# Gated cross-attention block: staging part of one unit's rows earlier, and adding a mask by VectorE

## What is computed

```python
ln = layernorm(latents)              # the 512 rows; xn is the same of the 32 context rows
q = (ln @ Wq), kv = concat([xn @ Wkv, ln @ Wkv])      # 16 heads of 64
sim = einsum('bhid,bhjd->bhij', rmsnorm(q) * scale, rmsnorm(k))
sim = where(padded_mask, sim, -max)  # padded_mask: the context's mask, then ones for the own rows
out = einsum('bhij,bhjd->bhid', softmax(sim), v) ... @ Wout + bout
x = x + tanh(g_xattn) * out
x = x + tanh(g_ffn) * top2_experts(layernorm(x))      # 8 experts, two chosen for each row
```

## Time and profile before

| | us |
|---|---|
| three runs | 344.81, 341.92, 344.61 |
| median | 344.61 |
| the profiled execution's own time | 345.44 |
| its span (first to last instruction) | 343.5 |
| PE busy | 303.0 (88%) |
| DVE busy | 271.5 (79%) |
| POOL busy | 268.0 (78%) |
| ACT busy | 203.2 (59%) |

### The profile page before, as it was taken

The page is one execution under the profiler, slowest core; times in us unless marked ns, Lnnn a source line. Parts: engine busy times, 40 slices in busy tenths (PEclk is TensorE's granted clock), DMA queues, the critical chain, the costliest instruction groups (busy, mean ns, idle before and its releaser), DMA issues.

```text
span 343.5 us, 8712 instructions
## 1 busy us (share of the span) xinstructions
PE 303.0 (88%) x3321; PEld 185.0 (54%) x3321; DVE 271.5 (79%) x516; ACT 203.2 (59%) x353; POOL 268.0 (78%) x203
## 2 busy tenths in 40 slices
PE   0567588896999999999999999999988799999993
PEld 0233143454465555565555556688866575655552
DVE  3897868995698899899898876954827976898994
ACT  2463746764576656767755756466773466665551
POOL 8699886897498999999998996745983449677652
PEclk9996859997899999999999999999999999999997
DMA  6406322167310812613515429370100000001001
GB/s 175 143 1 141 62 31 44 33 149 167 75 44 16 179 46 44 157 36 78 126 35 127 93 55 252 67 221 29 40 10 2 1 3 0 2 3 31 2 0 32
DMA packets 33723, 23.62 MB, mean 69 GB/s; under 512 B 10834, under 2 KB 33170, under 8 KB 33682
## 3 DMA queue, kind: packets, MB, share of 16 engines
q1 hardware_dynamic: 32738, 23.03, 29.3%
q10 hardware_dynamic: 944, 0.04, 0.2%
HBM read 5.87 MB, written 0.52 MB: 19 GB/s over the span
## 4 chain that ended last, share of the span: by engine, by line
PE 59%; POOL 14%; issue 9%; DVE 9%; ACT 5%; DMA 2%; POOLq 0%; SPq 0%; DVEq 0%; ACTq 0%
PE big L1532 8%; PE big L1533 7%; POOL p_lo L634 7%; PE o_ps L1368 5%; PE big L1387 5%; PE o_ps L1362 5%; PE o_ps L1363 4%; PE pj L1339 4%; PE tv L1375 3%; POOL rms_r L498 2%; PE pj L1298 2%; DVE nm_main L997 2%; PE tv L1322 2%; PE pj L1299 1%; PE pj L1300 1%
## 5 line engine op out<-in xcount | busy, mean ns | idle before, releaser
L599 POOL TENSOR_TENSOR p_lo<-p 128x1024 f16<-128x1024 f32 x64 | 121.8, 1914 | 12.3 <-ACT p L795 12.3
L795 ACT ACTIVATE p<-big 128x1024 f32<-128x1024 f32 x64 | 65.6, 1025 | 46.3 <-PE big L1533 46.3
L997 DVE TENSOR_REDUCE nm_main<-big 128x2 f32<-128x1024 f32 x64 | 78.2, 1221 | 18.0 <-PE big L1387 17.1
L498 POOL TENSOR_TENSOR rms_r<-meansq,power 128x8 f32<-128x8 f32 x32 | 52.3, 1637 | 17.6 <-DVE meansq L971 17.5
L634 POOL TENSOR_TENSOR p_lo<-p,p_lo 128x512 f16<-128x512 f32 x32 | 37.1, 1159 | 30.3 <-ACT p_lo L876 29.4
L1532 PE MATMUL big<-w 128*128 128x512 f16 x128 | 49.3, 385 | 1.9 <-ACT p L795 1.6
L1533 PE MATMUL big<-w 68*128 68x512 f16 x128 | 49.2, 384 | 0.0
L1362 PE MATMUL o_ps<-v,p 128*128 128x65 f16 x512 | 40.7, 194 | 0.0
L1363 PE MATMUL o_ps<-v,p 128*128 128x64 f16 x512 | 40.6, 195 | 0.0
L1362 PEld LDWEIGHTS o_ps<-v,p 128*128 128x128 bf16 x512 | 35.9, 99 | 6.9 <-issue 3.9
L1363 PEld LDWEIGHTS o_ps<-v,p 128*128 128x128 bf16 x512 | 34.5, 98 | 3.3 <-issue 0.3
(11 more groups left out here) (228 smaller groups left out, 714.6 us busy)
## 6 DMA issues: line engine op xcount, KB each, us to landing
w<-hl SPq DMA_DIRECT2D x32, 256.0 KB, 4.1
w<-hl SPq DMA_DIRECT2D x32, 128.0 KB, 3.7
pc_st<-pc_hi SPq DMA_DIRECT2D x64, 32.0 KB, 1.9
pc_st<-pc_lo SPq DMA_DIRECT2D x32, 32.0 KB, 1.9
hl<-n_kernel_gating_EDF_dram SPq DMA_DIRECT2D x1, 1024.0 KB, 6.5
hl<-L_ffn_kernel_up_EDF_dram SPq DMA_DIRECT2D x1, 1024.0 KB, 5.5
o_sb<-in_L_xattn_Wkv_dram SPq DMA_DIRECT2D x2, 384.0 KB, 6.8
x_sb<-in_x_dram SPq DMA_DIRECT2D x2, 256.0 KB, 3.7
```

What stands on the lines that cost most here:

```text
L498: nc.gpsimd.tensor_tensor(rms_r[:, tau % QT, :], meansq[:, tau % QT, :], power[:, 0:8], ALU.pow).then_inc(rr_ok, 1)
L599: nc.gpsimd.tensor_tensor(p_lo[m % NP][:, :], p[m % NP][:, :], p_hi[m % NP], ALU.subtract).then_inc(plo_ok, 1)
L795: nc.scalar.activation(p[n % NP][:, :], st_ps, ACT.Exp).then_inc(exp_ok, 1)
L997: nc.vector.tensor_reduce(nm_main[:, u % 2, 2 * c:2 * c + 2, q], s2_ps.rearrange("p (k n) -> p k n", k=2), AX_X, ALU.max, negate=True).the ...
```

## The change

Two things change. SP stages unit 1's four DMAs of high halves in slot -1, ahead of the six of `Vst`; the four others, with low halves, are issued in slot 2 as before, behind the stack. And `context_scores` loses the product with the mask: the first of the eight products of 64 columns starts the bank, and DVE adds the mask in place in the bank ahead of its reduction, with a semaphore `cm_ok` between. For that the mask's row lies on all 128 partitions in 32 bits (its DMA reads it once for each partition), and the row of ones goes, with its memset on POOL.

```diff
-        mask_u8 = sb("mask_u8", [1, BC], U8)
-        mask_row = sb("mask_row", [1, B, C], BF16)
+        mask_u8 = sb("mask_u8", [P, BC], U8)
+        mask_row = sb("mask_row", [P, B, C], F32)
...
-        ones_row = sb("ones_row", [1, P], BF16)
...
-        W_AT = {(FIRST, 2)[u] if u < 2 else 8 * u - 8: u for u in range(UNITS)}
+        W_AT = {(FIRST, -1)[u] if u < 2 else 8 * u - 8: u for u in range(UNITS)}
+
+        W_LO_AT = {2 if u == 1 else n: u for n, u in W_AT.items()}
...
-            sp.dma_start(mask_u8[:, :], mask.rearrange("b c -> (b c)").unsqueeze(0)).then_inc(mask_in, 16)
+            sp.dma_start(mask_u8[:, :], mask.rearrange("b c -> (b c)").partition_broadcast(P)).then_inc(mask_in, 16)
...
                         sp.dma_start(w1[DH:P, 0:2, odd, :], hl[rows, 0, 0:2, :]).then_inc(w1_ok[u % 2], 16)
+                if n in W_LO_AT:
+                    u = W_LO_AT[n]
+                    w1, w2, hl = W1[u % 2], W2[u % 2], HL[u % 2]
                     need_lo(sp, QT * (u + 1))
...
-            nc.gpsimd.memset(ones_row[:, :], 1.0)
...
             def context_maxima(u):
                 dve.wait_ge(cs_ok, u + 1)
+                if u == 0:
+                    dve.wait_ge(mask_ok, 1)
+                sc = o_ps[0][:, :].rearrange("p (k c) -> p k c", c=C)
+                nc.vector.tensor_tensor(sc, sc, mask_row[:, batch(u), :].unsqueeze(1).broadcast_to([P, HG * QT, C]),
+                                        ALU.add).then_inc(cm_ok, 1)
+                dve.wait_ge(cm_ok, u + 1)
...
                 else:
-                    pe.wait_ge(mask_ok, 1)
                     pe.wait_ge(kc2_ok, 2)
-                nc.tensor.matmul(o_ps[0][:, :].rearrange("p (k c) -> p k c", c=C), ones_row[:, :],
-                                 mask_row[:, batch(u), :].unsqueeze(1).broadcast_to([1, HG * QT, C]), start=True, stop=False,
-                                 skip_group_check=True)
...
-                                                start=False, stop=True, skip_group_check=True)
+                                                start=c == 0 and q == 0, stop=True, skip_group_check=True)
```

More of the change, by code:

```diff
@@ L207, in flamingo_gated_block @@
         pcst_ok = [sem(f"pcst_ok{h}") for h in range(HG)]
-        kc2_z, kc2_ok = sem("kc2_z"), sem("kc2_ok")
+        kc2_z, kc2_ok, cm_ok = sem("kc2_z"), sem("kc2_ok"), sem("cm_ok")
         def need(eng, s, count):
```

## The result

The changed kernel takes 338.58 us as the median of four runs (338.50 to 338.94), beside 344.06 us for the kernel before (four runs, 341.92 to 344.81). The ratio is 0.9838, with a 95% interval of 0.9804 to 0.9871: 1.6% faster. The profiled execution took 338.54 us with a span of 336.7 us, 6.8 less than the 343.5 before.

What follows compares the result with a forecast made beforehand. PE was taken to bound the kernel from about 85 to 210 us, after a 3.01 us hole. Gains 5.71 + 0.2 + 0.3 + 0.19 - 0.35 = 6.05 us from the 344.61 median gave 338.6 us, range 335.6 to 342.0.

Steps and rivals of the forecast that it cites:

- Staging, -5.71 us: At PE's hole from 80.41 us: earlier high-half DMAs save 5.71 us, 3.01 of idling and 2.70 of low clock.
- The margin of 0.2 us: Unit 3's high halves on ACT: the last staging DMA lands at 78.5 us, 0.2 us before ACT is ready at 78.67.
- the rival of a hole left over: Part of the second rival: 1 us of hole stays at 80 us, 339.6 with the clock kept, 342.3 without.
- Mask in units 3 to 5, -0.07 each: Slot 13 and its counterparts: of PE's 0.42 us only 0.07 is left per unit at the projection into `pj`.
- Mask in unit 2, -0.07: Slot 13: the same 0.07 us gain as units 3 to 5, with DVE's pair still starting at 103.57 us.
- Unit 6, -0.19: L1418 alone decides there, comes 0.23 us late, and 0.19 of PE's 0.42 us is kept.
- Unit 7, +0.35: L1418 has 0.44 us to spare and comes 0.77 late, so PE's 0.42 becomes a loss of 0.35 us.
- Unit 1, 0: First slots, where DVE sets the pace: no mask gain taken, between 0 and 0.42 us.
- Unit 0, -0.2: Product in a stretch of clock 0.52: a gain of 0.2 us taken, between 0 and 0.5.
- The first (DVE hides all): Rival: PE keeps 0.42 us in all seven units after unit 0, 8.85 us gained, 335.8 us; chance 0.09.
- The second: Rival: the hole at 80 us stays wholly (344.3 us) or as 1 us (339.6 or 342.3); chance 0.14.
- The third: Slower rival: the mask addition is held up beside POOL, 0.76 us more each; 343.2 us, 348.6 or 359 with low clock; chance 0.05.

Runs made afterwards that it cites:

- the repetition: The changed kernel run again with no edit: 338.44 us beside 344.34 for the kernel before, ratio 0.9827.
- Staging alone: The kernel before with only unit 1's four high-half DMAs moved to slot -1, the mask still PE's product: 339.37 us, ratio 0.9843.
- mask alone: The changed kernel with all eight staging DMAs of unit 1 in slot 2 again: 343.79 us, ratio 0.9988.
- half of the staging: The changed kernel with two of unit 1's four high-half DMAs moved back behind the stack: 339.83 us, ratio 0.9875.
- product in unit 7: The changed kernel with the mask made by PE's product again in unit 7 alone: 339.05 us, ratio 0.9855.
- turned later: The changed kernel with PE's turning of the maxima, and ACT's copy of the result, one step later: 341.88 us, ratio 0.9920.
- no mask in the maxima: The changed kernel without DVE's mask addition and without PE's product, so context row maxima are taken unmasked: 337.50 us, ratio 0.9796.
- mask added twice: The changed kernel with DVE's mask addition, semaphore included, made two times: 344.63 us, ratio 1.0009 to the kernel before.
- addition in SBUF: The changed kernel with one more DVE addition of the same size, all in SBUF and read by nobody: 345.81 us, ratio 1.0019.

## Why the prediction was right, and where not

The forecast was 338.6 us, and 338.58 was measured. That it is so near is in part luck. The forecast gain was 6.0 us from a median of 344.61; with the fourth run that median is 344.06, and the measured gain is 5.5, or 5.9 (344.34 - 338.44) in the repetition. In the two profiles of the changed kernel slots 0 to 60 are 5.3 and 5.9 us shorter than before, so the profiles can't decide between them. The staging was right as a mechanism and in size; the mask's small terms are right in part, and unit 2 and unit 7 spoil their sum. Point by point:

**Staging, -5.71 us**, from the same instructions eight slots later. Staging alone gives -5.70 (5.20 and 0.50). The hole, the ACT wait behind it and the landing as its cause are confirmed by mask alone and by half of the staging. The margin of 0.2 us was mis-sized: it is 2.0 us, and 1.0 in the second profile. The working let the last DMA land 5.3 us behind its issue as before, and it took 4.0; so the rival of a hole left over was further away than I thought. The low clock behind a hole is no fixed price: 2.7 us before, 1.5 us in mask alone, none behind a hole of 1.0 us. The sum took it from one execution; by the medians, staging alone brings 5.0 us (344.34 - 339.37).

**Mask in units 3 to 5, -0.07 each.** Measured -0.10. PE's 0.42 us is confirmed to the hundredth (24.16 - 23.74), so the 0.10 beyond the product's own 0.32 is real; that it goes on the change of rows, or on the drain that the prediction cites for it, no run shows separately. DVE's 0.73 is, too: 0.72 from start to start, and 0.73 for a second one. So is the 0.06 us that the working put, without a row, between DVE's merge and PE: 0.05 in unit 2 (99.18 - 99.13) and 0.06 in unit 7 (220.06 - 220.00). The working went in two steps, 0.19 kept at the turning and 0.07 at the projection into `pj`; measured are 0.19 (0.42 less the 0.23 of slot 22) and 0.10. Only what I said would be seen was wrong: no idle time of 0.35 us stands before the projection. By the working itself only 0.12 would be left there, as 0.23 is lost at L1423; the trace of unit 3 shows 0.15 us of idle time before L1423, and the projection starts 0.42 us behind the first of its slot's scores (124.96 - 124.54), where 0.32 is usual (79.64 - 79.32).

**Mask in unit 2, -0.07.** Here a step failed: I read DVE's time of 103.57 us from a trace in which the hole stood ahead of it. Without the hole DVE is 0.30 us later there, for POOL, and the unit became 0.21 us longer than with the staging alone (24.38 - 24.17). That the removal of a hole moves everything behind it by the same amount, on every engine, was the tacit assumption; POOL "keeps pace, with little to spare" was written down and not followed up.

**Unit 6, -0.19.** Measured -0.24 and -0.25 in the changed kernel, but -0.09 in mask alone and with the product in unit 7, which have the same addition in it; what makes the 0.15 us between them stays open. **Unit 7, +0.35.** L1418, now L1423, is late (0.79 us of idle time against 0.77 foretold, and 0.5 in the other profile), but what that costs can't be told: slots 48 to 60 take 40.36 to 41.14 us with the addition (turned later left out), 40.79 with the product there, 40.44 and 40.55 with neither. Only staging alone and before have 40.17 and 40.18. The wait for the stack's DMA ahead of it, from none to 1.3 us in the profiles, hides a term of 0.35. **Unit 1, 0.** Measured -0.07. **Unit 0, -0.2**: the start of slot 0 scatters by more.

**The mask's part together.** I had 0.34 us of gain. Without slots 0 and 48 to 60, the table gives -0.08 + 0.21 - 0.30 - 0.25 = -0.4, and slots 48 to 60 give back 0.2 to 0.8: nothing that can be measured. The change is faster for its staging alone. In the profiled executions 0.84 us of the 6.8 fell into the rest and 0.62 ahead of slot 0, where no edit shows; with them the parts add up.

**The rivals.** The first (DVE hides all) is refuted: what it would look like is no mask in the maxima, 0.32 us less for each of units 3 to 5. The second is what half of the staging shows in part, with its clock kept. The third has a real mechanism, but not at this place: the addition took 0.69 us all eight times, even beside `p_lo`. The Trainium skill (SBUF — State Buffer, SBUF: two separate sides) has it so: VectorE and GpSimd share a pair of ports as an exclusive lock, taken by a VectorE operation with two SBUF inputs against a GpSimd operation that reads SBUF, for the whole instruction. The trace agrees for `p_lo` (held up until 0.54 us behind its end), and for the mask's addition, with one SBUF input; it disagrees for `rms_r`, which reads two SBUF tiles and beside which the SBUF addition took 0.69 us.

The Trainium skill's rule on the drain (VectorE: DVE Perf Modes, The DRAIN you can't avoid), which I had set against the trace, would have made the reduction start 0.69 us later instead of 0.73. The prediction made too much of the difference: the same section adds that a next operation which isn't held starts earlier, so a start ahead of the end is no disagreement. Only the price of the semaphore is one: 0.73 us for an addition with a semaphore behind it (mask added twice) and 0.60 without (addition in SBUF), where the section has it cost nothing extra.

## What to carry to other kernels

A wait on a transfer is to be traced to the queue that issues it: moving 3 us of issues ahead of a burst of 8 us brought all of the gain here. When a hole is removed, look at what else it sheltered: an engine at 98% of the pace (POOL, 23.68 of 24.17 us) has no rest left, and the waits it brings appear some slots later, on another engine. Moving work from the bounding engine to one at 90% pays only as far as the receiving engine has room in the very slot, and leaving the work out (0.42 us a unit) was worth four times as much as moving it (0.10) in units 3 to 5.

## What the runs showed of the hardware

- A hole of 1.0 us of PE, and the waits of 0.84 to 1.27 us that units 2 to 6 have where the mask is added twice, left the granted clock at 1.00; behind holes of 3.0 and 3.3 us it was low, for 2.7 and 1.5 us of lost time.
- A VectorE addition with all operands in SBUF takes 0.69 us, or ends 0.54 us behind a GpSimd subtraction of 1024 elements that it meets (so 1.60 us in slot 5); with one operand in PSUM it takes 0.69 in both cases. Beside GpSimd's power instruction of 8 elements (1.64 us) nothing is held up.
- It works both ways: a GpSimd subtraction that starts just behind the SBUF addition took 2.35 or 2.15 us instead of 1.89.
- The time from the issue of one DMA to its landing isn't fixed: the last staging DMA of unit 1 took 5.3 us before, 4.0 and 4.1 in the two profiles of the changed kernel, and 5.2 with half of the staging moved back.
